# Expert layer of a two-layer decoder: the weights' rests moved from GpSimd to VectorE, the marks' kind, and the place of the owners' load

## The reference, cut to what matters

```python
def _L0_ffn_ref(x, norm_weight, gate_w, w1, b1, w2, b2):
    t = x * rsqrt(mean(x * x, axis=-1) + RMS_EPS) * norm_weight   # x is _layernorm(x) of the layer's input
    tokens = t.reshape(-1, D)                                     # 4096 x 256
    gate_logits = tokens @ gate_w.T                               # 4096 x 8
    gate_scores, expert_idx = top_k(gate_logits, 2)
    routing_weights = softmax(gate_scores)
    combine = zeros((T, E)).at[arange(T)[:, None], expert_idx].add(routing_weights)
    # for every expert: h = gelu(tokens @ W1.T + B1); o = h @ W2.T + B2; acc += c[:, None] * o
    return x + out
```

## Time and profile before

| | us |
|---|---|
| median of 3 executions | 3734.63 (3733.24 to 3734.75) |
| the profiled execution, its time | 3770.42 |
| the profiled execution, its span | 3768.7 |
| TensorE matmul busy (PE) | 3535.4 (94%) |
| VectorE busy (DVE) | 2815.1 (75%) |
| ScalarE busy (ACT) | 2067.1 (55%) |
| GpSimd busy (POOL) | 460.0 (12%) |

### The profile page before, as it was taken

How to read it: one execution, slowest core, us unless ns; L and a number is a source line. 1 busy time by engine, 2 the same in 40 slices (tenths; PEclk the granted TensorE clock), 3 DMA queues, 4 the chain that set the end, 5 groups by cost and what they waited for, 6 DMA issues and landing times. The chain is left out here.

```text
span 3768.7 us, 92062 instructions
## 1 busy us (share of the span) xinstructions
PE 3535.4 (94%) x28674; PEld 2949.1 (78%) x28674; DVE 2815.1 (75%) x8955; ACT 2067.1 (55%) x6494; POOL 460.0 (12%) x599
## 2 busy tenths in 40 slices
PE   8999999899999999489967989999799999999999
PEld 6888888788888887389945666666688888888887
DVE  7666666677777776766657977888788888888886
ACT  6777777677777776335534648888433223232232
POOL 0000000000000000435578002222000000000000
PEclk9999999999999999689989999999899999999999
DMA  2000000110000000312211000000300000000000
GB/s 103 0 0 0 0 0 0 40 35 11 11 11 11 11 11 12 129 50 77 73 59 45 0 17 20 22 22 17 105 9 14 11 8 17 8 14 11 8 14 9
DMA packets 48158, 96.08 MB, mean 25 GB/s; under 512 B 7584, under 2 KB 21280, under 8 KB 47776
## 3 DMA queue, kind: packets, MB, share of 16 engines
q1 hardware_dynamic: 40640, 75.48, 6.0%
q0 software_dynamic: 6528, 17.83, 1.6%
q10 hardware_dynamic: 864, 1.19, 0.1%
HBM read 72.46 MB, written 22.02 MB: 25 GB/s over the span
## 5 line engine op out<-in xcount | busy, mean ns | idle before, releaser
L2416 DVE TENSOR_TENSOR f_zgT<-f_zT,f_ps_g 128x512 fp32r<-128x512 f32 x512 | 327.4, 681 | 15.4 <-PE f_ps_g L2248 11.4
L718 ACT ACTIVATE c_pr<-c_sm,c_nmx 128x256 f32<-128x256 f32 x512 | 254.5, 499 | 148.7 <-DVE c_nmx L550 148.7
L148 PE MATMUL f_ps_out<-f_out_rounded,f_zgT 128*128 128x256 f32 x1024 | 295.4, 288 | 1.3 <-DVE f_zgT L2416 1.3
L149 PE MATMUL f_ps_out<-f_out_rest,f_zgT 128*128 128x256 f32 x1024 | 289.4, 283 | 0.0
L150 PE MATMUL f_ps_out<-f_out_rounded,f_zgT 128*128 128x256 f32 x1024 | 288.0, 281 | 0.0
L2369 DVE TENSOR_TENSOR f_gv<-f_ps_v,f_gm 128x512 f32<-128x512 f32 x256 | 175.6, 686 | 143.1 <-PE f_ps_v L150 142.9
L718 ACT ACTIVATE a_pr<-a_sm,a_nmx 128x128 f32<-128x128 f32 (+1 forms) x512 | 227.1, 444 | 99.6 <-DVE a_nmx L550 99.6
L550 DVE CUSTOM_DVE_ANT_0 a_sm<-a_ps_s,causal 128x128 f32<-128x128 f32 (+1 forms) x512 | 152.3, 354 | 152.8 <-PE a_ps_s L416 152.8
L550 DVE CUSTOM_DVE_ANT_0 c_sm<-c_ps_s,c_mask 128x256 f32<-128x256 f32 x512 | 186.5, 420 | 87.9 <-PE c_ps_s L416 87.7
L2505 ACT ACTIVATE f_pr<-f_sm,f_nmx 128x128 f32<-128x128 f32 (+1 forms) x256 | 114.9, 449 | 193.2 <-DVE f_nmx L2389 193.2
L2514 ACT COPY f_prT<-f_ps_t 128x256 f32<-128x256 f32 x128 | 47.8, 373 | 287.3 <-PE f_ps_t L2217 287.3
(11 more groups left out here) (422 smaller groups left out, 11523.5 us busy)
## 6 DMA issues: line engine op xcount, KB each, us to landing
f_slot_out<-f_y SPq DMA_DIRECT2D x72, 128.0 KB, 1.7
c_ctx_stage<-in_ctxT SPq DMA_DIRECT2D x32, 256.0 KB, 2.8
f_w_whole<-in_f_w SPq DMA_DIRECT2D x15, 512.0 KB, 5.1
x_sb<-in_x SPq DMA_DIRECT2D x8, 512.0 KB, 7.3
c_mask_stage<-in_mask SPq DMA_DIRECT2D x16, 256.0 KB, 3.0
f_token_rows<-f_t SPq DMA_DIRECT2D x16, 256.0 KB, 3.3
x_mid<-x_sb SPq DMA_DIRECT2D x16, 256.0 KB, 2.0
f_xn<-x_mid SPq DMA_DIRECT2D x16, 256.0 KB, 2.6
```

Of the source, the lines that this page charges most:

```text
L148: nc.tensor.matmul(out, sh, mh, start=start, stop=False, **kw)
L149: nc.tensor.matmul(out, sh, ml, start=False, stop=False, **kw)
L718: last = nc.scalar.activation(pr[:, r, i, 0:n], sm[:, j, i, 0:n], ACT.Exp, bias=nmx[:, j, i:i + 1], scale=-1.0, accum_out=sums[:, r, i:i + 1])
L2416: last = nc.vector.tensor_tensor(zgT[:, k % 2, r], zT[:, s % 2, r, :].bitcast(F32).unsqueeze(1).broadcast_to([P, 2, S]), ps_g[:].rearrange ...
```

## The change

Four things change in `routed_experts`. VectorE writes the weights' rests, one piece in each batch of the gates from batch 2 on and the last two behind the batches, and ScalarE rounds one piece a batch in step with it; GpSimd's waits and its sixteen subtractions are gone. `hot_row` and `hot_tile` have the kind float32r; the first comparison is written to a plain float32 tile `marks`, which has the same place in memory as `hot_tile`, and the multiplication reads it and writes `hot_tile`. Two small tiles of the later steps (`tile_no`, `owner_f`) are views of `marks`. The owners are loaded after step 43 instead of 49, and on each engine behind its work on the first tile's rows.

```diff
-        hot_row = sb("hot_row", [P, 2, GROUP, P], F32, choosing)
-        hot_tile = sb("hot_tile", [P, 2, GROUP, NT], F32, choosing)
+        hot_row = sb("hot_row", [P, 2, GROUP, P], F32R, choosing)
+        marking = ExitStack()
+        marks = sb("marks", [P, 2, GROUP, NT], F32, marking)
+        marking.close()
+        hot_tile = sb("hot_tile", [P, 2, GROUP, NT], F32R, choosing)
...
-            eng.wait_ge(made, CHOICES)
+            eng.wait_ge(made, OWNED)
...
-            pool.wait_ge(t_ready, B)
-            pool.wait_ge(pieces.split, 1)
-            pieces.rest_by_pool(nc, pool, 1, len(pieces.list))
...
-            regs, owner_of = owners(pe)
-            pe.wait_ge(pieces.split, len(pieces.list))
-
             def turn_rows(n):
...
+            turn_rows(0)
+            regs, owner_of = owners(pe)
+            pe.wait_ge(pieces.split, len(pieces.list))
...
             for b in range(B):
                 rest_tT(b)
+                if b >= 2:
+                    pieces.rest(nc, dve, b - 1, b)
                 if b + 2 < B:
                     normalise(b + 2)
+            pieces.rest(nc, dve, B - 1, len(pieces.list))
...
-                nc.vector.tensor_tensor(hot_tile[:, g % 2], each(tile_of[:, at], NT), every(block_no[:], NT),
+                nc.vector.tensor_tensor(marks[:, g % 2], each(tile_of[:, at], NT), every(block_no[:], NT),
                                         ALU.is_equal).then_inc(tile_hot, 1)
...
-                nc.vector.tensor_tensor(hot_tile[:, g % 2], hot_tile[:, g % 2], each(token_no[:, token], NT),
+                nc.vector.tensor_tensor(hot_tile[:, g % 2], marks[:, g % 2], each(token_no[:, token], NT),
                                         ALU.mult).then_inc(hot_ready, 1)
...
-            regs, owner_of = owners(dve)
-
...
             rest_x(0)
+            regs, owner_of = owners(dve)
...
-                if b % 2:
-                    pieces.round(nc, act, 1 + b // 2, 2 + b // 2)
+                if b >= 2:
+                    pieces.round(nc, act, b - 1, b)
             take_lT(B - 1)
+            pieces.round(nc, act, B - 1, len(pieces.list))
...
-            pieces.round(nc, act, 1 + B // 2, len(pieces.list))
-
-            regs, owner_of = owners(act)
...
             round_x(0)
+            regs, owner_of = owners(act)
```

More of the change, by code:

```diff
@@ L815, in routed_experts @@
         slot_f = sb("slot_f", [P, Q], F32, choosing)
-        tile_no = hot_row[:, 1].rearrange("p g m -> p (g m)")[:, 0:NT * (E - 1)].rearrange("p (n e) -> p n e", e=E - 1)
-        owner_f = hot_tile[:, 1, 0, :]
+        tile_no = marks[:].rearrange("p a g n -> p (a g n)")[:, 0:NT * (E - 1)].rearrange("p (n e) -> p n e", e=E - 1)
+        owner_f = marks[:, 1, 0, :]
         power = sb("power", [P, WORDS, PER], F32, choosing)
@@ L870, in routed_experts @@
         CHOICES = 49
-        SLOTS, PLACED = 37, 38
+        SLOTS, PLACED, OWNED = 37, 38, 43
         xt = lambda n: c.x[:, n:n + 1, :].rearrange("p a d -> p (a d)")
@@ L1063, in second @@
                 last.then_inc(y_ps, 1)
-            turn_rows(0)
             for n in range(NT + 2):
@@ L1208, in _ @@
             done(nc.vector.tensor_copy(owner[:], word_f[:]))
+            assert k == OWNED, k
             done(nc.vector.tensor_copy(slot_at[:].rearrange("p r n -> p (r n)"), slot_f[:]))
```

## The result

The changed kernel takes 3709.47 us (median of 4, 3707.44 to 3710.53) where the kernel before takes 3734.46 in the same comparison: a ratio of 0.9931, 95% interval 0.9918 to 0.9944, so 25 us or 0.7% less. In the ratio's own terms that is 25.8 us, with 20.9 and 30.6 as the ends of the interval. Two later comparisons of the same two kernels gave 0.9923 (0.9909 to 0.9936) and 0.9933 (0.9919 to 0.9946).

The account below looks back on a forecast made before the run. Three chained stages before the loop: no engine full in the gates, VectorE bounds the choice, TensorE the marks. -25.1 + 6.1 + 2.8 - 8.3 - 1.3 = -25.8 from 3734.6 gives 3709 us, own range 3704 to 3714.

Parts of the forecast that it names:

- choice: Stage after the gates: without GpSimd's subtractions beside them, VectorE's elementwise instructions shorten from 32.9 to 7.8 us, -25.1 us.
- batches 2 to 15: Gates: VectorE takes one rest a batch, so the step grows from 2.36 to 2.8 us, +6.1 us.
- end of the gates: From the last line 1109 to the choice: ScalarE's last two roundings and the last rest add +2.8 us (2.5 to 3.5).
- marks: Stage after the choice: one record a product instead of two, so VectorE binds at 2.47 us a group, -8.3 us.
- start of the loop: Before the first product: the first tile's rows are turned before the owners are loaded, -1.3 us (0 to -2.2).
- Rival 3: Choice: GpSimd does not hold up VectorE, so the main term is gone; 3734 us, chance 0.02.
- the chain: Gates: norms, transposes, gates, copy, rounding and rest in sequence over two batches, 5.9 us, so 2.95 a batch.
- Rival 1: Gates: piece arrival, store of t and lower clock add up instead of hiding, +14.8 for +6.1; 3718 us, chance 0.17.
- rival 4: Gates: the new chain closes over one batch, not two, step 5.9 us, +46 for +6.1; 3749 us, chance 0.03.
- a step over 3.3 us: Gates: a step between batches longer than this would show the prediction wrong.
- The clock: Gates: granted 0.77, taken as about half at 1.2 GHz; the skill's rule would keep 2.4 GHz and give +3.1 us.
- Rival 2: Marks: the rounded kind brings nothing at 72 columns, so the marks stay TensorE's; 3717 us, chance 0.08.

Follow-up runs that it names:

- no_rests: The kernel before without the sixteen rests on any engine, TensorE multiplying by the rounded weights a second time instead; ratio to before 0.9927.
- waits_again: Changed kernel with norms ahead of each piece's rest and the last two rests in VectorE's waits, a repeat; 3733.9 us, ratio to before 0.9917.
- owners_only: The kernel before with only the owners loaded after step 43 and behind each engine's first tile, two helper tiles moved to hot_tile; ratio 0.9992.

## Why the prediction was right

The time, 3709.5 us, was within a microsecond of the 3709, which is partly luck in the sum: the traces of before and after differ by 27.3 us in this layer and not by 25.8, and the medians by 25.0, with 21 and 31 as the ends of the interval.

| step | predicted | trace |
|---|---|---|
| choice | -25.1 | 18.9 - 44.2 = -25.3 |
| batches 2 to 15 | +6.1 | 35.9 - 30.7 = +5.2 |
| end of the gates | +2.8 | 6.0 - 2.8 = +3.2 |
| marks | -8.3 | 21.9 - 30.2 = -8.3 |
| start of the loop | -1.3 | 6.9 - 8.6 = -1.7 |
| batches 0 to 2 | 0 | 4.1 - 4.5 = -0.4 |

The rows hold two single profiles. With the means of all profiles that have the same code in a stage the batches are 35.6 - 30.0 = +5.6, the end 5.7 - 2.7 = +3.0 and the choice 18.9 - 43.9 = -25.0.

- *GpSimd holds up VectorE.* Right, and shown by no_rests, which has 18.9 us where the prediction had 19: the times of the earlier trace rows were enough to price it. Rival 3 is gone.
- *The gates.* Right in kind and a little too dear. I took 2.8 us a batch, between VectorE's 2.6 and the chain's 2.95. The trace has 2.57 wherever VectorE does not wait, and the chain shows only as waits for ScalarE's roundings, 2.5 us in these thirteen steps. Of these 0.9 stand behind the late arrival of the pieces 12 to 16, for which ScalarE waits 1.0: that term, one microsecond, was right. Taking the chain away (waits_again) gives 33.3 us for the thirteen steps, which is the VectorE bound of the prediction, 33.8 less the missing norms. With the spread of equal gates the term is anything from 4.5 to 6.6 us, so that 6.1 was too dear is not shown. Rival 1, +14.8, is out, and so is rival 4, whose step was 5.9. The prediction's own sign of being wrong, a step over 3.3 us, was set too low: two steps are 3.5 (batches 2 to 3 and 13 to 14), and the mean is 2.8.
- *The clock.* The stage is at 0.75 after 0.77. By the rule that the prediction names, from the Trainium skill, TensorE: Matmul & The Clock Gate, section "HAM oscillation — how this bites in real kernels", it would have stayed at the upper level; it did not. The price of the lower one was small even so, since in the steps of 2.57 us VectorE has no wait.
- *End of the gates.* The order of ScalarE's work is as worked out; the last two rests wait 0.8 us for the roundings.
- *Marks.* Right in every part: one record a product, VectorE's pitch 2.48, 2.0 us of tail. The 27.3 us over which the prediction took TensorE's pitch are 27.6 in the earlier trace rows, 0.216 us for 0.213, which changes nothing. Rival 2 is out.
- *Owners.* The mechanism was right, the size low: the first turning waited for the rows' transfer and not for the load, and it came 4.15 us behind the row numbers, where I had 1626.2 - 1622.15 = 4.05. From there to the first product I had 3.2 us, the turning, the load and 0.6 of register work one behind another. The load starts with the turning and not behind it (both at 1601.2), and the product follows at 1603.94, 2.8 us later. The prediction said that no memory moves; in fact `tile_no` had to leave `hot_row`, in owners_only too, because the early first tile could be written over what VectorE still reads. That follows from the program's order of memory; no run has it the other way.
- *Profile and median.* The 35.8 us between the profiled execution of before and its median I took for a matter that would not touch the difference. It did not. Some 30 of them are the unchanged stage, if the profile was taken on a chip like the one where before took 3765 to 3769 us; which chip it was is not on record.

## What to carry to other kernels

Find an instruction that occurs twice with one shape, once beside another engine's work and once alone: the pair prices the contention, and the grouped mean hides it. Work moved off a stalled engine should be set against the idle time of where it goes, but with the waits that it adds itself: a piece's rest put ahead of what feeds the pipeline costs more than behind it, and waits for another engine's last result are the cheapest places, unless something is released by it that gets in the way of what comes next (here the next layer's loads, 0.3 to 0.4 us). Before comparing two profiles, subtract stages that nothing changed: here that was half of the difference.

## What the runs showed of the hardware that was not expected

VectorE's norms, tensor_scalar of 128x256 from SBUF to SBUF with per-partition operands, are held up by GpSimd's subtraction until it ends (a pair takes 2.5 to 2.7 us for 0.73), as are two-input instructions; I had expected only the latter to matter in the gates. A GpSimd fill holds up no two-input instruction (0.42 and 0.43 us beside it) but does hold up a tensor_scalar of 128x8 (0.47 for 0.17). One product of the rounded kind with 72 moving columns is one record of 407 ns, against two of 421 before, at the lower clock; records overlap, and eight of them take 1.92 us. The `remote` waits of ScalarE in the long stage, 11 to 13 of them with the longest 4.0 to 5.2 us, come on one chip in every profile and not on the other; what they wait for stays open.
